# Q and every other fill drawn from one pool of five PSUM banks, waits of Q and scores split by pass, and a new order

## The reference

```
h = group_norm(x, 8 groups)                     # per image and group of 16 channels
q, k, v = h @ qkv_w.T + qkv_b                   # 1024 tokens of 128 channels
x = x + softmax(q @ k.T / sqrt(128)) @ v @ proj_w.T + proj_b

u = layer_norm(x, over channels) * norm_g + norm_b
z, xBC, dt = split(u @ in_w.T)                  # 128, 128+64+64, 4
xs, B, C = split(silu(causal_conv4(xBC) + conv_b))
dt = softplus(dt + dt_bias);  A = -exp(A_log)
state = state * exp(dt * A) + dt * xs (x) B     # over 1024 tokens, 4 heads of 32
y = (state . C + Dp * xs) * silu(z)
out = rms_norm(y) * rms_w @ out_w.T
x = x + out * sigmoid(se2(relu(se1(mean(out)))))
```

## Time and profile before

| | us |
|---|---|
| runs, median (lowest, highest) | 275.69 (275.29, 276.14) |
| the profiled execution | 275.25 |
| its span, first to last instruction | 273.1 |
| TensorE busy in it | 256.9 |
| VectorE busy | 224.8 |
| ScalarE busy | 208.5 |
| GpSimd busy | 109.0 |

### The profile page before, as it was taken

The page is one execution under the profiler, slowest core; times in us unless marked ns, Lnnn a source line. Parts: engine busy times, 40 slices in busy tenths (PEclk is TensorE's granted clock), DMA queues, the critical chain, the costliest instruction groups (busy, mean ns, idle before and its releaser), DMA issues. The chain is left out here.

```text
span 273.1 us, 6193 instructions
## 1 busy us (share of the span) xinstructions
PE 256.9 (94%) x1992; PEld 224.3 (82%) x1992; DVE 224.8 (82%) x517; ACT 208.5 (76%) x414; POOL 109.0 (40%) x114
## 2 busy tenths in 40 slices
PE   2999999999999999999999998999999999998791
PEld 2889998998888998989989787888889788677680
DVE  5787765754889799889988999999899999599933
ACT  2356579978999887879999875777978888997261
POOL 8030032208053300642387534132463188556162
PEclk9999999999999999999999999999999999999996
DMA  6930000006000600000326000060007201000014
GB/s 175 397 136 4 0 0 4 0 5 186 8 0 6 183 12 2 0 2 0 112 78 206 0 2 1 16 182 2 0 5 189 84 0 42 0 2 1 0 41 155
DMA packets 10987, 15.29 MB, mean 56 GB/s; under 512 B 1515, under 2 KB 5708, under 8 KB 10956
## 3 DMA queue, kind: packets, MB, share of 16 engines
q1 hardware_dynamic: 10412, 14.69, 16.7%
q10 hardware_dynamic: 544, 0.21, 0.3%
HBM read 12.70 MB, written 2.20 MB: 55 GB/s over the span
## 5 line engine op out<-in xcount | busy, mean ns | idle before, releaser
L1157 PEld LDWEIGHTS attn_out<-values,pT 128*128 128x128 f32 x512 | 63.3, 191 | 5.8 <-issue 4.0
L1157 PE MATMUL attn_out<-values,pT 128*128 128x129 f32 x512 | 66.7, 276 | 0.0
L974 DVE TENSOR_REDUCE neg_max<-scores 128x1 f32<-128x1024 f32 x32 | 39.0, 1218 | 16.0 <-PE scores L1157 15.8
L649 ACT ACTIVATE probs<-scores,neg_max 128x512 f32<-128x512 f32 x64 | 41.8, 685 | 13.1 <-DVE neg_max L974 11.1
L655 ACT ACTIVATE pT<-turn 128x512 f32<-128x512 f32 x64 | 37.6, 595 | 10.8 <-PE turn L1230 10.8
L1230 PE MATMUL turn<-ident,probs 128*128 128x128 f32 x256 | 37.1, 273 | 0.0
L575 POOL TENSOR_TENSOR pre<-pre,th 128x512 f32<-128x512 f32 x16 | 21.4, 1336 | 30.0 <-ACT pre L681 18.3
L1230 PEld LDWEIGHTS turn<-ident,probs 128*128 128x128 f32 x256 | 30.2, 142 | 2.9 <-issue 0.7
L1157 PE MATMUL scores<-h_hi,q_hi 128*128 128x512 f32 x64 | 30.4, 474 | 0.0
L1067 DVE TENSOR_TENSOR_SCAN L<-L,ident 128x512 f32<-128x512 f32 x24 | 29.9, 1256 | 0.0
L561 POOL TENSOR_TENSOR ln_rstd<-ln_var,neg_half 128x4 f32<-128x4 f32 x8 | 9.8, 1230 | 47.6 <-DVE ln_var L996 47.5
(11 more groups left out here) (219 smaller groups left out, 592.4 us busy)
## 6 DMA issues: line engine op xcount, KB each, us to landing
L<-decay_rows_d SPq DMA_DIRECT2D x24, 256.0 KB, 3.9
res<-in_x_tok SPq DMA_DIRECT2D x4, 512.0 KB, 7.8
out<-res SPq DMA_DIRECT2D x8, 256.0 KB, 2.7
x_all<-in_x SPq DMA_DIRECT2D x3, 512.0 KB, 8.5
decay_in<-decay_rows_d SPq DMA_DIRECT2D x24, 64.0 KB, 3.5
x_all<-in_x SPq DMA_DIRECT2D x2, 256.0 KB, 3.2
winT<-in_in_wT SPq DMA_DIRECT2D x1, 194.0 KB, 7.2
wqkv<-in_qkv_w ACTq DMA_DIRECT2D x1, 192.0 KB, 4.1
```

What stands on the lines that cost most here:

```text
L649: act.activation(probs[:, i % 2, half_of(h)], scores[:, half_of(h)], ACT.Exp, bias=neg_max[:, i:i + 1]).then_inc(exp_done.sem, 1)
L974: V.tensor_reduce(neg_max[:, n:n + 1], scores[:, :], AX.X, ALU.max, negate=True).then_inc(max_ready.sem, 1)
L1157: return T.matmul(o, w, v, start=start, stop=stop)
```

## The change

It has five parts.

1. The head. The masks become a step of the table, `masks`, in two pieces: the first (identity copies, centring matrix) stays at the front, the second (row masks) is placed behind the first row maximum. DVE's wait for all constants goes. Between the two averaging products two steps stand instead of four, since the product now reads the averaged mean from PSUM and a fused instruction squares and adds. gn_bias takes one instruction instead of two for image a, three for the others, off a negated mean that is made beside the second product.
2. Waits pass by pass. `Q` waits for h's high part, does both passes that need no more, then waits for the low part and does the third. `S` waits for q_hi, does high x high and high x low of h, then waits for q_lo.
3. `Q` fills a bank of its own and no longer the score pair; so it doesn't wait for the last image's last exp, which `S` now waits for.
4. The pool: `turn` and `mamba` become five banks for every fill, `Q` and the weight products included.
5. `ORDER` is new, in places and banks.

Two lines of the table, where image a begins:

```
-warm3 gn_stats0 gn_mm10 kq_mm gn_dev0 gn_mm20 kq_ev gn_ve0 vp_mm gn_pow0 gn_aff0 h0a h1a warm5 h_hi0a h_hi1a h_lo0a
+masks0 gn_stats0 warm3 gn_mm10@4 kq_mm@0 gn_dev0 gn_mm20 gn_ve0 kq_ev warm5 gn_pow0 gn_aff0 h_hi0a h0a h1a h_lo0a
```

The core of the rest:

```diff
-        turn = [ctx.enter_context(nc.psum_tensor(f"turn{k}", [P, HALF], F32)) for k in range(2)]
-        mb = [ctx.enter_context(nc.psum_tensor(f"mamba{k}", [P, HALF], F32)) for k in range(3)]
+        pool_banks = [ctx.enter_context(nc.psum_tensor(f"bank{k}", [P, HALF], F32)) for k in range(5)]
...
         def fill(pe, b, kind, n):
-            uses, memory = (TURN_USES, turn) if kind in ("V", "T") else (MAMBA_USES, mb)
+            uses, memory = USES, pool_banks
             bank, before = uses[kind, n, b]
             if before is not None:
...
+                for read, batch, count in released(*before):
+                    wait(pe, read, batch, count)
...
-            dve.wait_ge(consts_done.sem, 9 + TERMS)
...
-                    step_done(V.tensor_copy(gn_mean[:, b0:b1], mb[2][:, b0:b1]))
-                    step_done(V.tensor_tensor(gn_dev[:, b0:b1], gn_mv[:, b0:b1, 0], gn_mean[:, b0:b1], ALU.subtract))
-                    step_done(V.tensor_tensor(gn_dev[:, b0:b1], gn_dev[:, b0:b1], gn_dev[:, b0:b1], ALU.mult))
-                    V.tensor_tensor(gn_dev[:, b0:b1], gn_dev[:, b0:b1], gn_mv[:, b0:b1, 1], ALU.add
-                                    ).then_inc(gn_dev_done.sem, 1)
+                    bank = take(dve, 0, "gn_mm1", n)
+                    step_done(V.tensor_tensor(gn_dev[:, b0:b1], gn_mv[:, b0:b1, 0], bank[:, b0:b1], ALU.subtract))
+                    if n == 0:
+                        V.scalar_tensor_tensor(gn_sq[:, 0:1], gn_dev[:, 0:1], gn_dev[:, 0:1], gn_mv[:, 0:1, 1], ALU.mult, ALU.add
+                                               ).then_inc(gn_dev_done.sem, 1)
...
                 if kind == "Q":
-                    wait(pe, exp_done, b - 1, 15 + n)
-                    wait_h_lo(pe, b, n + 1)
                     wait(pe, h_hi_ready, b, n + 1)
                     pe.wait_ge(kq_ready.sem, 1)
-                    mm3(scores[:, half], key_query_hi[:, :], key_query_lo[:, :], h_hi[:, half], h_lo[:, half]
-                        ).then_inc(Q_filled.sem, 1)
+                    bank, done = fill(pe, b, "Q", n)
+                    mm(bank[:, :], key_query_hi[:, :], h_hi[:, half], True, False)
+                    mm(bank[:, :], key_query_lo[:, :], h_hi[:, half], False, False)
+                    wait_h_lo(pe, b, n + 1)
+                    mm(bank[:, :], key_query_hi[:, :], h_lo[:, half], False, True).then_inc(done, 1)
...
                     if i == 0:
-                        wait(pe, q_lo_ready, b, h + 1)
+                        wait(pe, q_hi_ready, b, 1)
+                        wait(pe, exp_done, b - 1, 15 + h)
                     else:
                         wait(pe, exp_done, b, n - 1)
+                        wait(pe, q_hi_ready, b, i // QUAD + 1)
+                    wait(pe, h_hi_ready, b, h + 1)
+                    mm(to, q_hi[:, tile(i)], h_hi[:, keys], True, False)
+                    wait_h_lo(pe, b, h + 1)
+                    mm(to, q_hi[:, tile(i)], h_lo[:, keys], False, False)
                     wait(pe, q_lo_ready, b, i // QUAD + 1)
-                    wait_h_lo(pe, b, h + 1)
-                    mm3(scores[:, half_of(h)], q_hi[:, tile(i)], q_lo[:, tile(i)], h_hi[:, half_of(h)],
-                        h_lo[:, half_of(h)]).then_inc(S_filled.sem, 1)
+                    mm(to, q_lo[:, tile(i)], h_hi[:, keys], False, True).then_inc(S_filled.sem, 1)
```

More of the change, by code:

```diff
@@ L68 @@
[L68 to L72, removed]
@@ L149, with bank_uses @@
 STEPS = [parse(s) for s in ORDER]
-def bank_uses(turn):
+def bank_uses():
     last, uses = {}, {}
     for kind, n, b, bank in STEPS:
-        if bank is not None and (kind in ("V", "T")) == turn:
+        if bank is not None:
             uses[kind, n, b] = bank, last.get(bank)
@@ L378, in fill @@
         def fill(pe, b, kind, n):
-            uses, memory = (TURN_USES, turn) if kind in ("V", "T") else (MAMBA_USES, mb)
+            uses, memory = USES, pool_banks
             bank, before = uses[kind, n, b]
             if before is not None:
-                reads = bank_read[before[0]]
-                if before[0] == "Out":
-                    reads = [(o_ready, 1)] if before[2] < BATCH - 1 else [(o_raw_ready, 1)]
-                if before[0] == "Cum" and not by_dma(before[2]):
-                    reads = reads + [(dA_ready, 1)]
-                if before[0] == "DAT" and by_dma(before[2]):
-                    reads = [(rows_ready, 1)]
-                last_only = before[0] in ("DAT", "Dec", "L") and not by_dma(before[2])
-                for read, each in reads:
-                    wait(pe, read, 0 if read is o_raw_ready or last_only else before[2], each * (before[1] + 1))
+                for read, batch, count in released(*before):
+                    wait(pe, read, batch, count)
@@ L635, in step @@
                 elif kind == "q_hi":
-                    wait(act, Q_filled, b, n + 1)
+                    bank = take(act, b, "Q", n)
                     wait(act, S_filled, b - 1, 8 * n + 8)
-                    act.activation(q_hi[:, half], scores[:, half], ACT.Identity, bias=col[:, QA:QA + 1]
+                    act.activation(q_hi[:, half], bank[:, :], ACT.Identity, bias=col[:, QA:QA + 1]
                                    ).then_inc(q_hi_ready.sem, 1)
@@ L969, in step @@
                     wait(dve, q_hi_ready, b, n + 1)
-                    V.scalar_tensor_tensor(q_lo[:, half], scores[:, half], col[:, QA:QA + 1],
+                    bank = take(dve, b, "Q", n)
+                    V.scalar_tensor_tensor(q_lo[:, half], bank[:, :], col[:, QA:QA + 1],
                                            q_hi[:, half].bitcast(F32), ALU.add, ALU.subtract).then_inc(q_lo_ready.sem, 1)
@@ L1180, in prepare @@
                     pe.wait_ge(vec_in.sem, 16)
-                    mm(turn[0][:, 0:P], wqkv[:, 0, :], wqkv[:, 1, :])
-                    mm(turn[0][:, P:P + 1], wqkv[:, 1, :], vec[:, QB:QB + 1]).then_inc(kq_filled.sem, 1)
+                    bank, done = fill(pe, 0, "kq_mm", 0)
+                    mm(bank[:, 0:P], wqkv[:, 0, :], wqkv[:, 1, :])
+                    mm(bank[:, P:P + 1], wqkv[:, 1, :], vec[:, QB:QB + 1]).then_inc(done, 1)
                 elif kind == "vp_mm":
```

276 lines of the change are left out of this document (151 added, 125 removed).

## The result

The changed kernel takes 271.39 us (median of four, 271.19 to 272.00) against 275.72 for the kernel before: 0.9847 of it, 95% interval 0.9825 to 0.9869. The forecast was 274.1 and its range began at 271.5, 0.1 above what was measured. Faster was right; the gain is 4.3 us instead of 1.6.

What follows compares the result with a forecast made beforehand. TensorE was taken to bound 20 to 155.4 us, VectorE the last image's scores, small steps the last 11.3 us. Terms: -0.8 + 0.3 + 0.8 - 1.5 = -1.2, thus 274.05; predicted 274.1 us, range 271.5 to 276.9.

Steps and rivals of the forecast that it cites:

- the middle: 20 to 155.4 us, TensorE always busy: one of four close T waits on shared banks, +0.3 us.
- the last image: Scores, 155.4 to 216.3 us: VectorE gets 1.9 us more work, partly taken up by idle time, +0.8 us.
- Waits of Q and S: Splitting the waits of Q and the scores by pass costs sequencer instructions alone; costed at nothing.
- Head: Before 20 us: Q at 10.9 instead of 11.98, first row maximum 0.8 us earlier, bounds 0.4 to 1.1.
- The third rival: Head not shortened, since warm and weight products stand ahead of Q: 274.85 us, chance 0.06.
- The second rival: Shared pool makes TensorE wait on images two to four, 0.33 us each; 277.05 us at ten waits, chance 0.15.
- The first rival: VectorE takes the head's gain back, all 1.9 us in the last image: 275.15 us, chance 0.24.
- End: After the last row maximum: same VectorE work but for 0.3 us, other pieces in its holes, -1.5 us.
- Its parts: Last maximum to last inverse -0.5, to end of dA_head +0.2, to first state scan -0.9, to last y -0.3 us.
- sp_den's hole: VectorE's wait at sp_den for its exponential, between last inverse and dA_head, kept at about 1.0 us.
- the end's better bound: After the last row maximum: holes cannot shrink below 1.6 us, so 3.5 at best; the range used -3.0.
- Hidden waits: Waits inside TensorE's stream of products that reads as busy; costed at nothing, chance 0.03.

Runs made afterwards that it cites:

- e2: Changed kernel, but each Q and score tile waits for its low part (h_lo, q_lo) before its first pass: 273.07 us, 0.9902 of before.
- e10: Kernel before, with only Q's pass with h_lo put last and alone waiting for h_lo; the scores' waits left: 275.66 us, 1.0000 of before.
- e1: Kernel before with its own order and waits, only the banks handed out anew over all five: 276.16 us, 1.0016 of before.
- e6: Kernel before, with GpSimd's wide element-wise instructions of images 3 and 4 cut to one eighth of their columns: 273.77 us.
- e3: Changed kernel with its order, but banks split again: value products and T on two, all others on three: 306.65 us.
- e7: Changed kernel, with GpSimd's wide element-wise instructions of images 3 and 4 cut to one eighth of their columns: 269.62 us.
- e12: e4 without the ten passes of warm products between the second averaging product and Q: 271.71 us, 0.9845 of before.
- e4: Changed kernel with six more warm products in front, the first nine waiting for the identity alone: 270.84 us, 0.9826 of before.
- e8: e4 plus one warm product ahead of each of the last image's two pooling and two channel products: 270.89 us.
- e9: Kernel before with six more warm products in front, the first nine waiting for the identity alone: 275.18 us, 1.0001 of before.

## Why the prediction was right in sign and short by 2.7 us

Two steps failed, both between the first and the last row maximum, where the sum had +0.3 for the middle and +0.8 for the last image, thus +1.1, and the traces show -1.6. That is off by 2.7 us, as much as the forecast is in all.

**Waits of Q and S, forecast 0, measured -1.0 us in the traces and -1.5 in the times (e2).** This is the first step that failed: "That waits of Q and S are split costs instructions of the sequencer alone ... I cost it at nothing." I looked only at what splitting adds, and in the trace of before nothing waits there. What it takes away is a constraint on the order: in the new one Q stands so close behind its input that the wait for h_lo costs 0.3 to 0.5 us at images 2 and 4. e10 shows that the same edit of Q is worth nothing in the old order; it is worth its 1.5 us with the order that uses it.

**Head, forecast -0.8.** Every start up to Q was met within 0.2 us. From Q to the first maximum I used durations of the earlier trace rows, taken when TensorE was already fast; in the changed kernel's trace it ran at the low level until 13.22, so only 0.11 us is left in this pair of traces. With the head of before the level rose at 11.98, 13.82 and 14.28 (before, e1, e6), with the new head at 13.22, 11.30 and 10.44 (changed, e3, e7), and the first row maximum ended at 18.08 and 16.76 on average. Three traces each are too few to say whether the change itself moves the rise. Compared at the same level the new head ends about 0.65 us sooner (an estimate, on straight lines between the traces: 16.83 for 17.46 at a rise at 11.98, 17.35 for 18.01 at 13.22). The difference of the medians, -4.33, less -1.58 and -1.55 of the two later stretches of the traces, leaves -1.2 for the head. So the term was of the right size as far as is known, 0.65 to 1.2, for all that this pair shows 0.11. The third rival's time looks met in this one trace, but its cause isn't: Q starts right behind the last weight product, as that rival has it, and still 1.25 us earlier than before, at 10.73.

**Middle, forecast +0.3 for T in the shared pool.** Nothing of the kind: e1 has 201.53 us between the maxima against 201.49, and in the changed kernel no wait of T is named. The second rival is out in this order; e3 shows what it looks like when it is true. (Both traces record 1992 matmul instructions; the prediction's 1295 stands in neither, but that the number stays is so.)

**Last image, forecast +0.8.** This is the second step that failed, and the larger: of the -1.58 us between first and last maximum 1.0 are the waits of Q and S, and 0.6 the rest of the change (e2 against before), where +1.1 stood in the sum. The additional q_lo, xs and xdt are there (122 instructions against 120 between the maxima), about 1.9 us of VectorE's time as forecast, but no cost of them shows: with GpSimd's instructions cut the stretch is 59.0 us for 59.2 (e7, e6), and with them 2.5 us shorter. I used mean durations of whole lines and did not see that the 58.37 us of VectorE in the earlier trace rows held 3.1 us of waiting on GpSimd inside its instructions. Most of these moved to the third image, so the last image by itself is no measure of the whole. Of the 0.6 us up to 0.4 go with the hold-ups (1.7 against 1.3 for the cut in e6 and e7); what the remainder is, and why the additional work shows no cost, stays open. The first rival is out.

**End, forecast -1.5, measured -1.55.** Its parts were -0.5, +0.2, -0.9, -0.3 and came out at -0.36, -0.34, -0.46, -0.39. The sum is right partly by offsets: sp_den's hole closed to 0.3 where I kept 1.0, and the scan came 6.22 after dA_head, not 5.8, with GpSimd busy for 6.01 of it, as the prediction had feared. VectorE's idle time is 2.8 us of 41.04 where 3.5 was forecast. In the range the prediction put the end's better bound at -3.0 where it had worked out 3.5, and 274.1 starts from the profiled execution (from the median the same sum gives 274.5); neither makes up the miss.

**Hidden waits, chance 0.03.** These are waits in TensorE's stream of products that reads as busy. The prediction cost them at nothing, and no run shows them at the size of a rival: the middle took 136.60 us with 120.29 of weight loads, against 135.40 with 120.59 before, and the shortest stretch between the maxima of all runs, 198.58 in e7, is 2.9 us below that of before. In small they exist: a TensorE that reads as busy throughout can wait, 0.3 us at Q in e2, and only the starts show it.

## What to carry to other kernels

A wait that does not show in the trace before can still be worth removing, if a new order leans on its absence; test parts in the order in which they will stand. Read TensorE's starts, not its busy time, and VectorE's shortest duration of a form, not its mean: what lay between in the last image was waiting for a neighbour, and went from 3.1 to 0.4 us when the neighbour's instructions were cut. A profile of a head that begins at the low clock level is one draw; compare several before sizing an edit there.

## What was not expected of the hardware

- Ahead of the first rise the view shows a granted clock of 1.00 although products take as long as they do where it reads 0.50 (a Q pass 0.63 us at 11.31 in the changed kernel, where the view reads 1.00, and at 10.19 in e12, where it reads 0.50); so the low level must be read from durations there.
- After a start at 4.74 to 4.83 us the level rose between 10.44 and 14.28, by up to 2.8 us apart in three traces of the same head; with a start at 1.86 or 1.87 it rose at 5.0 to 5.4 (e4, e8, e12), and in e9 between 5.66, where a 128-column product still takes 0.39 us, and 6.97. Both falls in the head, in e9 at 9.3 us (granted clock 0.65 from 9 to 10) and in e12 at 8.9 (0.95 from 8 to 9), came after gaps in TensorE's products, 1.10 us between starts at 5.66 and 1.51 us idle ahead of 8.72. What sets the level, and why equal heads differ, no run here shows.
- Small operations of VectorE are held up by a GpSimd instruction beside them too: in the kernel before a product sp_s, 0.15 us at its shortest, took 0.81 at 194.11 us, 0.77 of it beside a residual add.
